# A two-layer graph-attention kernel: x transposed by VectorE flips instead of TensorE, its low part on GpSimd, the adjacency read directly, and new instruction orders

## The reference, cut to what matters

```python
# layer 0: q, k, v = x@Wq.T, x@Wk.T, x@Wv.T + bv
scores = einsum('bqhd,bkhd->bhqk', q, k) * 384**-0.5 + (adj + adj)
p = softmax(where(any(scores != 0, -1), scores, -inf)); p = nan_to_num(p)
x = layernorm(x + (p @ v) @ Wo.T + bo)
# layer 1: q, k, v = x@Wq + bq, x@Wk + bk, x@Wv + bv
scores = einsum('bhqd,bhkd->bhqk', q, k) / sqrt(32) + beta * adj
p = softmax(where(adj > 0, scores, -9e15))
out = layernorm(x + p @ v)
```

## Time and profile before

| what | value |
|---|---|
| median of 3 runs | 2175.8 us (2172.58 to 2176.5) |
| the profiled execution, its own time | 2174.43 us |
| its span, first to last instruction | 2172.6 us |
| PE busy | 2073.7 us, 95% |
| DVE busy | 1859.6 us, 86% |
| ACT busy | 1838.6 us, 85% |
| POOL busy | 1564.2 us, 72% |
| mean share of the DMA engines | 54.8% |

### The profile page before, as it was taken

How to read it: one execution, slowest core, us unless ns; L and a number is a source line. 1 busy time by engine, 2 the same in 40 slices (tenths; PEclk the granted TensorE clock), 3 DMA queues, 4 the chain that set the end, 5 groups by cost and what they waited for, 6 DMA issues and landing times.

```text
span 2172.6 us, 86873 instructions
## 1 busy us (share of the span) xinstructions
PE 2073.7 (95%) x23808; PEld 1911.8 (88%) x23808; DVE 1859.6 (86%) x8451; ACT 1838.6 (85%) x7688; POOL 1564.2 (72%) x2188
## 2 busy tenths in 40 slices
PE   5899999999999999999999999999999999999974
PEld 4799989999999999999999999999998999999963
DVE  2588888998898998898898888898889899889874
ACT  4489888888888888888988888988888988888874
POOL 3667777777777777777777777777777777777752
PEclk8899999999999999999999999999999999999986
DMA  4255565565565565555556556556555556556544
GB/s 124 64 133 143 137 152 144 137 153 135 137 153 135 137 152 140 135 149 144 136 144 153 130 142 154 139 137 153 136 138 153 144 135 152 137 137 153 128 120 105
DMA packets 234778, 300.33 MB, mean 138 GB/s; under 512 B 26704, under 2 KB 226384, under 8 KB 234576
## 3 DMA queue, kind: packets, MB, share of 16 engines
q1 hardware_dynamic: 234576, 298.43, 54.8%
HBM read 46.67 MB, written 25.17 MB: 33 GB/s over the span
## 4 chain that ended last, share of the span: by engine, by line
PE 74%; DVE 11%; issue 8%; POOL 3%; DMA 1%; DVEq 1%; ACT 1%; SPq 0%; POOLq 0%; ACTq 0%
PE r_bank L371 18%; PE r_bank L373 17%; PE r_bank L372 17%; PE s_bank L421 9%; PE r_bank L437 7%; DVE neg_s L699 4%; PE r_bank L354 2%; PE r_bank L449 2%; DVE neg_max L699 1%; DVE x1T_lo L721 1%; PE r_bank L364 1%; DVE flip L715 1%; DMA prob0T<-flip 1%; DVE v L776 1%; DVE sum_neg L748 1%
## 5 line engine op out<-in xcount | busy, mean ns | idle before, releaser
L594 ACT ACTIVATE prob<-neg_s,neg_max 128x128 f32<-128x128 f32 x3072 | 1190.7, 393 | 98.6 <-DVE flip L715 82.0
L699 DVE CUSTOM_DVE_ANT_0 neg_s<-s_bank,bias 128x128 f32<-128x128 f32 x3072 | 668.3, 285 | 67.4 <-PE s_bank L421 64.4
L594 ACT ACTIVATION_READ_ACCUMULATOR prob<-neg_s,neg_max 128x1 f32 x3072 | 592.5, 193 | 0.0
L928 POOL TENSOR_TENSOR prob<-prob,inv_sum 128x512 f32<-128x512 f32 x384 | 389.4, 1042 | 223.6 <-DVE inv_sum L787 223.6
L371 PE MATMUL r_bank<-xT_hi,w_hi 128*128 128x256 f32 x1152 | 328.7, 285 | 20.9 <-DVE xT_lo L721 19.4
L371 PE MATMUL r_bank<-x1T_hi,w_hi 128*128 128x256 f32 x1152 | 337.2, 293 | 10.5 <-DVE x1T_lo L721 8.3
L373 PE MATMUL r_bank<-xT_hi,w_lo 128*128 128x256 f32 x1152 | 327.6, 284 | 0.0
L372 PE MATMUL r_bank<-xT_lo,w_hi 128*128 128x256 f32 x1152 | 327.4, 284 | 0.0
L373 PE MATMUL r_bank<-x1T_hi,w_lo 128*128 128x256 f32 x1152 | 325.5, 283 | 0.0
L372 PE MATMUL r_bank<-x1T_lo,w_hi 128*128 128x256 f32 x1152 | 324.9, 282 | 0.0
L910 POOL TENSOR_TENSOR flip<-neg_s 128x768 f32<-128x768 f32 x128 | 234.9, 1835 | 95.0 <-DMA prob0T<-flip 94.9
(11 more groups left out here) (82 smaller groups left out, 5242.2 us busy)
## 6 DMA issues: line engine op xcount, KB each, us to landing
prob0T<-flip SPq DMA_DIRECT2D x512, 192.0 KB, 3.5
prob1T<-stage SPq DMA_DIRECT2D x512, 192.0 KB, 3.6
x_in<-in_x_dram SPq DMA_DIRECT2D x128, 192.0 KB, 3.6
x_late<-x SPq DMA_DIRECT2D x64, 384.0 KB, 4.2
out_dram<-y SPq DMA_DIRECT2D x128, 192.0 KB, 2.4
adj<-in_adj_dram SPq DMA_DIRECT2D x256, 64.0 KB, 2.4
stage<-in_L_gnn_Wv_dram SPq DMA_DIRECT2D x1, 576.0 KB, 5.7
stage<-in_L_gnn_Wq_dram SPq DMA_DIRECT2D x1, 576.0 KB, 6.6
```

The costliest lines, as they stand in the source:

```text
L594: act.activation(prob[layer][:, h, :], neg_s[layer][:, h, :], ACT.Exp, bias=neg_max[layer][:, h:h + 1], scale=-1.0, accum_out=row_sum[laye ...
L699: dve.tensor_tensor_reduce(neg_s[layer][:, h, :], s_bank[b][:, (h // HC) * N:(h // HC + 1) * N], bias[layer][q.parity][:, g, :], -1.0, BIG ...
L928: pool.tensor_tensor(prob[0][:, hs, :], prob[0][:, hs, :], inv_sum0[:, hs].unsqueeze(2).to_broadcast([P, HC, N]), ALU.mult).then_inc(probn ...
```

## The change

- x is loaded twice. The copy for the residual goes straight into x_bo and bo is added in place. The copy for the transposition goes into x_q: partition block i (32 partitions) holds features 96i to 96i+95 of tokens in blocks of 32, in pieces of 96 floats. DVE transposes its 32x32 blocks into xT, and this is the full transpose. The three weights of layer 0 that multiply x are loaded with their rows in the matching order, two of them from ACT's queue.
- The six transposes of x per body leave PE; two flips of 128x384 join DVE (`flip_x`). ACT's high part reads xT in SBUF with a stride, and the low part (`low_xT`) moves from DVE to POOL, with a strided read too.
- The bias of layer 0 is no longer made: `negate` reads adj with the factor -2, and q is scaled by half.
- RING_USERS loses xt0 and xt1, so it has 26 names, which is no multiple of four, and all orders of work are new. On PE the attention of layer 0's first graph, attend(0, n, 0), moves from the start of the next body to the end of this one. The loop covers bodies 9 to 60.
- Weights are staged in other buffers; POOL splits three of them, at the end of body 0.

```diff
-FIRST, LAST = -1, PAIRS + 3
-LOOP_FROM = 7
-LOOP_N = PAIRS - 1 - LOOP_FROM
+FIRST, LAST = -2, PAIRS + 4
+LOOP_FROM = 9
+LOOP_N = PAIRS - 3 - LOOP_FROM
...
+RING_USERS = ["g1_0", "v0_1", "wo_0", "g1_1", "ot_0", "pv1_1", "v1_0", "g1_2",
+              "g0_0", "g1_3", "g1_4", "pv0_1", "ot_1", "v1_1", "g0_1", "g1_5",
+              "wo_1", "g0_2", "g0_3", "g0_4", "x1t0", "g0_5", "v0_0", "x1t1",
+              "pv0_0", "pv1_0"]
 RING = 4
-assert len(RING_USERS) % RING == 0
...
+            def load_q(q):
+                if q.valid():
+                    sp.wait_ge(xflip_done, q.count(1, 0, 0))
+                    for i in range(NB):
+                        sp.dma_start(x_q[HD * i:HD * (i + 1), :, :],
+                                     x[bass.ds(2 * q.index(), 2)].rearrange("g (j a) d -> a (g j) d", j=NB)[:, :, QD * i:QD * (i + 1)]
+                                     ).then_inc(xq_loaded, 16)
...
+                spread_probs(1, m4, 1)
+                store(m5, 1)
+                load_x(n)
                 spread_probs(0, m1, 1)
+                load_adj1(m1)
...
                     load_adj0(p1)
+                keep_x1(m3)
                 spread_probs(1, m3, 0)
+                store(m4, 0)
+                load_q(p3)
                 spread_probs(0, n, 0)
...
# PE, the whole body as it is now
                 scores(0, n, 0, r)
                 project_qk(1, m2, 0, r)
                 project_v(0, n, 1, r)
                 project_out0(m1, 0, r)
                 project_qk(1, m2, 1, r)
                 transpose_out1(m4, 0, r)
                 scores(1, m3, 1, r)
                 attend(1, m4, 1, r)
                 project_v(1, m2, 0, r)
                 project_qk(1, m2, 2, r)
                 project_qk(0, p1, 0, r)
                 project_qk(1, m2, 3, r)
                 project_qk(1, m2, 4, r)
                 attend(0, m1, 1, r)
                 transpose_out1(m4, 1, r)
                 scores(0, n, 1, r)
                 project_v(1, m2, 1, r)
                 project_qk(0, p1, 1, r)
                 project_qk(1, m2, 5, r)
                 project_out0(m1, 1, r)
                 project_qk(0, p1, 2, r)
                 project_qk(0, p1, 3, r)
                 project_qk(0, p1, 4, r)
                 transpose_x1(m1, 0, r)
                 scores(1, m2, 0, r)
                 project_qk(0, p1, 5, r)
                 project_v(0, p1, 0, r)
                 transpose_x1(m1, 1, r)
                 attend(0, n, 0, r)
                 attend(1, m3, 0, r)
...
# ACT, the end of the body
+                exps(0, n, 1, 8, 10)
                 qk_out(0, p1, 4, r)
+                norm_apply0(m1, 1)
+                exps(1, m2, 0, 0, 2)
                 qk_out(0, p1, 5, r)
                 high_x1T(m1, 1)
+                exps(0, n, 1, 10, 12)
+                high_o0T(n, 0)
...
# DVE, the start and the end of the body
                 inverse_sums0(m1, 1)
                 low_o0T(m1, 0)
                 negate(0, n, 0, (0, 1, 2, 3))
                 flip_probs(0, m1, 1)
...
                 negate(1, m2, 0, (0, 1, 2, 3))
+                values_out(0, p1, 0)
+                low_x1T(m1, 1)
+                abs_max(n, 1)
...
+            def flip_x(q, g):
+                if q.valid():
+                    dve.wait_ge(xq_loaded, q.count(8 * NB, 1, 8 * NB))
+                    dve.wait_ge(xt_lo_done, q.plus(-1).count(1, g, 1))
+                    dve.transpose(xT[:, :, g * N:(g + 1) * N].rearrange("p c (j a) -> p c j a", j=NB),
+                                  x_q[:, g * NB:(g + 1) * NB, :].rearrange("p j (c b) -> p c j b", c=C)
+                                  ).then_inc(xflip_done, 1)
...
# POOL, the body as it is now
                 normalise0(m1, 1)
+                residual0(m1, r)
+                low_xT(p1, 0)
+                low_xT(p1, 1)
                 residual1(m4, 0)
+                inverse_std(0, m1, 0)
+                fold_scores0(n, 0)
                 inverse_std(1, m4, 0)
                 normalise0(n, 0)
+                make_bias1(m1, 0)
                 residual1(m4, 1)
                 inverse_std(0, m1, 1)
+                make_bias1(m1, 1)
+                fold_scores0(n, 1)
                 inverse_std(1, m4, 1)
+                if is_peeled(r, off, 0):
+                    low_weights(WQ1, WK1, WV1)
```

More of the change, by code:

```diff
@@ L32 @@
 NB = N // HD
+QD = D // NB
 PAIRS = NG // 2
@@ L139, in build @@
         neg_half = sb("neg_half", [P, 1])
-        x_in = [sb(f"x_in{b}", [P, 2, D]) for b in range(2)]
+        x_q = sb("x_q", [P, 2 * NB, QD])
         x_bo = [sb(f"x_bo{b}", [P, 2, D]) for b in range(2)]
@@ L144, in build @@
         adj1 = sb("adj1", [P, 2, N])
-        bias = [[sb(f"bias{l}_{b}", [P, 2, N]) for b in range(2)] for l in range(2)]
+        bias1 = [sb(f"bias1_{b}", [P, 2, N]) for b in range(2)]
         qT = [[sb(f"q{l}T_{b}", [P, C, G2]) for b in range(2)] for l in range(2)]
@@ L279, in load_weights, with load_rows @@
                              ).then_inc(w_loaded[i], 16)
-            load_x(Pair(0, 0))
-            load_weights(WV0)
-            load_weights(WQ0)
+            def load_rows(i):
+                for k in range(NB):
+                    sp.dma_start(w_stage[i][HD * k:HD * (k + 1), :, :],
+                                 wts[i][QD * k:QD * (k + 1), :].rearrange("(c b) o -> b c o", c=C)).then_inc(w_loaded[i], 16)
+            load_q(Pair(0, 0))
+            load_rows(WV0)
             for layer, b_ in enumerate((bv0, bv1)):
                 sp.dma_start(bv_row[layer][:], b_.partition_broadcast(P)).then_inc(bv_loaded, 16)
-            load_weights(WK0)
             load_adj0(Pair(0, 0))
@@ L332, in _ @@
         def _(pe):
-            read = [(xt_lo_done, 0, 0, 0, 0)] * 4
+            read = [(v_out[0], 0, 0, 0, 0)] * 4
             s_read = [(neg_done[0], 0, 0, 0, 0)] * HC
@@ L346, in after_loop @@
                         table[i] = (sem_, off - 2, per, g, plus)
-            def transpose_x(q, g, r):
-                if q.valid():
-                    pe.wait_ge(*last_read(read, BANK[f"xt{g}"], r))
-                    read[BANK[f"xt{g}"]] = (xt_lo_done, q.off, 1, g, 1)
-                    pe.wait_ge(x_loaded[q.parity], q.loads(2))
-                    for c in range(C):
-                        mm = pe.transpose(ring(f"xt{g}")[:, c * P:(c + 1) * P],
-                                          x_in[q.parity][:, g, c * P:(c + 1) * P], ident[:])
-                    mm.then_inc(xt_done, 1)
             def transpose_x1(q, g, r):
@@ L607, in body @@
+                exps(1, m3, 0, 4, 8)
+                high_xT(p1, 0)
+                exps(1, m3, 0, 8, 10)
+                high_xT(p1, 1)
+                if is_peeled(r, off, -1):
+                    high_weights(WO0)
                 qk_out(1, m2, 0, r)
-                exps(1, m3, 0, 6, 12)
+                exps(1, m3, 0, 10, 12)
+                exps(0, n, 0, 0, 4)
                 qk_out(1, m2, 1, r)
-                exps(0, n, 0, 0, 4)
+                exps(0, n, 0, 4, 6)
+                out1T_out(m4, 1)
@@ L796, in body @@
                 n = Pair(r, off)
-                m4, m3, m2, m1, p1 = (n.plus(-4), n.plus(-3), n.plus(-2), n.plus(-1), n.plus(1))
-                values_out(0, n, 0)
-                low_x1T(m2, 1)
-                abs_max(m1, 1)
+                m4, m3, m2, m1, p1, p2 = (n.plus(-4), n.plus(-3), n.plus(-2), n.plus(-1), n.plus(1), n.plus(2))
                 inverse_sums0(m1, 1)
-                attention_out1(m4, 0)
                 low_o0T(m1, 0)
@@ L902, in make_bias1, with low_xT @@
                     pool.wait_ge(bias1_steps, q.count(3, g, 2))
-                    pool.tensor_tensor(bias[1][b][:, g, :], adj1[:, g, :], mask1[:], ALU.add).then_inc(bias1_steps, 1)
+                    pool.tensor_tensor(bias1[b][:, g, :], adj1[:, g, :], mask1[:], ALU.add).then_inc(bias1_steps, 1)
+            def low_xT(q, g):
+                if q.valid():
+                    pool.wait_ge(xt_hi_done, q.count(1, g, 1))
+                    if g == 0:
+                        pool.wait_ge(v_done[0], q.count(1, 0, 0))
+                        pool.wait_ge(g_done[0], q.count(3, 0, 0))
+                    m = slice(g * N, (g + 1) * N)
+                    pool.tensor_tensor(*(t.rearrange("p c (a j) -> p c a j", j=NB) if i != 1 else t.rearrange("p c (j a) -> p c a j", j=NB)
+                                        for i, t in enumerate((xT_lo[:, :, m], xT[:, :, m], xT_hi[:, :, m].bitcast(F32)))), ALU.subtract
+                                      ).then_inc(xt_lo_done, 1)
             def fold_scores0(q, g):
```

213 lines of the change are left out of this document (88 added, 125 removed).

## The result

The changed kernel takes 2480.0 us (2478.8 to 2480.7), the kernel before 2175.3 us on the same chip: 1.1405 times as long, 95% interval [1.1391, 1.1418]. The forecast was 2193 us.

What follows compares the result with a forecast made beforehand. PE was taken to bound the kernel: 31.77 us a body plus 1.12 us a turn. Bodies +11.4, turns +2.3 and start +4 gave +17.7 us on 2174.4, 2192.1, so forecast 2193 us; range 2148 to 2214.

Steps and rivals of the forecast that it cites:

- A new wait of PE: Over the body's end, project_qk(1, m2, 0) waits for low_o0T to read pv0_0's bank: 0.58 us per body.
- PE's own time: Six transposes per body leave PE, others get dearer: PE gains 0.39 us, not 0.72, body 31.38 us.
- The turn: DVE's standstill where the loop turns back costs 1.3 us instead of 1.12, 25 times instead of 27: +2.3 us.
- What costs nothing: Flips on DVE, strided high part on ACT, low parts on POOL, bias change: covered by idle time, bodies unchanged.
- pieces of x_q that hold up the spread: Rival: small x_q DMAs delay the spread, layer 0 sets the pace: some +60 us, 2253 us; chance 0.07.
- The adjacency: In layer 0, reading the bias straight from adj and halving q changes factors only; booked at nothing.
- The start: POOL's three weight splits delay the second flip to 66.3 us from 62.08: +4 us (0 to +7).

Runs made afterwards that it cites:

- banks by hand: The changed kernel with one edit: the four shared PSUM banks assigned to the 26 users by a written-out table that avoids the four clashes; 2176.5 us, 1.001.
- the predicted wait alone: Against the kernel with hand-assigned banks (2176.5 us): pv0_0 put back on g1_0's bank, x1t1 on bank 3 in exchange; 2186.8 us, 1.0044.
- the jump moved: The changed kernel with plain bank rotation, its jump by two moved from the body's end to project_out0(m1, 1) (wo_1); 2161.8 us, 0.9935.

## Why the prediction was wrong

Right in sign, far off in size: 18 us forecast, 304 measured. The step that failed is **"A new wait of PE"**. Its mechanism is right, and so is its size (0.63 us against 0.58). In the kernel that has it alone the path through ACT and DVE takes 3.44 us (1255.23 to 1258.67) where 3.46 was forecast, and PE's own steps 2.75 (1.87 us to 1257.10 and 0.88 for the scores) where 2.88 was forecast. The step failed in its reach: it took the rotation to be disturbed over the end of the body alone, where 26 is not a multiple of 4, and laid two paths side by side for that one pair of names. It did not go through the other pairs. But a rotation is only harmless if the orders of the readers fit it everywhere, and the change replaced both: the list of names and the orders of DVE and ACT. In the kernel before wo_1 followed g0_0 on its bank and g0_2 followed g1_3, both read by ACT; now they follow ot_1 and v1_1, which DVE reads late. What the prediction put at nothing by leaving it out, these two hand-overs, measured 1.8 and 1.1 us a body and, each alone, 134 to 163 and 96 us.

The account of the pair of bodies shown above, from the traces. PE's own work is 2 x 31.13 = 62.3 us. The waits are shown as 1.02, 0.43, 1.62 and 1.11 us in the first body and 0.63, 0.40, 1.86 and 1.11 in the second, 8.2 us. But a wait costs more than it shows. For g0_2 in the first body, the last start of PE ahead of the wait and the second start behind it lie 1.68 us apart (1257.15, 1258.83), where neighbouring rows have 0.29: 1.39 us for a wait shown as 1.11. Measured like this, from start to start, the eight waits cost 10.2 us (for the last the 1.39 of the first body is taken, since the clock was low). With 2.5 us for the clock the sum is 75.0 us, and 75.0 were measured.

Against the 64.4 us of the kernel with banks by hand the pair loses 10.6 us, and 30 pairs would make 318 us; measured were 304. Not every pair loses as much: the one from 336.59 to 408.61 takes 72.0 us, the clock is at 0.99 to 1.00 until 400 us, and later too a body now and then takes 36.00 us instead of 38.5 (895.19 to 931.19).

Step by step:

- **PE's own time**: forecast 31.38 us a body, measured 31.13 (above, at the predicted wait alone). The body of 31.44 us with banks by hand comes near the forecast by chance, because it holds 0.3 us of a hand-over. The transposes ahead of scores cost 0.42 and 0.48 us as taken from the earlier trace rows, but PE gains 0.64 us instead of 0.39; where the other 0.25 us come from is not traced.
- **The wait over the body's end**: 0.58 forecast, 0.63 measured, but it lengthens the body by only 0.38 us, and in a body with the turn it replaces a wait that would come later. The kernel that has this one of the four waits takes 2186.8 us. It is the kernel that the sum of the prediction describes (2193 us), and that the two are so near is in part luck: its plain body is 31.82 us instead of 31.96 and its turn 1.0 us instead of 1.3, while the start costs more than forecast.
- **The turn**: 1.3 us forecast. With banks by hand 1.52, with the jump moved 0.3: the standstill of DVE has no price of its own; it costs what PE waits for at the first thing that DVE owes. DVE's standstill lay where forecast, before the reciprocal, but came in two parts (timeline of DVE, banks):

```profile
1214.62 0.23 DVE L794 RECIPROCAL inv_raw<-row_sum 128x12 f32<-128x12 f32 x1 [0.64 <-issue]
...
1218.28 0.08 DVE L709 DVE_READ_ACCUMULATOR2_ANT neg_max<- 128x1 f32 x1 [0.63 <-issue]
```

- **What costs nothing**: the groups of the changed kernel, with the DMAs, next to the earlier trace rows:

```profile
L527 ACT ACTIVATE xT_hi<-xT 128x384 fp32r<-128x384 f32 x128 | 118.8, 931 | 87.5 <-PE r_bank L372 45.8 <-issue 39.5 <-DVE xT L737 2.1
L737 DVE STREAM_TRANSPOSE xT<-x_q 128x384 f32<-128x384 f32 x128 | 66.3, 555 | 6.4 <-DMA x_q<-in_x_dram 4.9 <-POOL xT_lo L914 1.4
L914 POOL TENSOR_TENSOR xT_lo<-xT,xT_hi 128x384 fp32r<-128x384 f32 x128 | 153.6, 1213 | 19.6 <-ACT xT_hi L527 17.4
```
```profile
x_q<-in_x_dram SPq DMA_DIRECT2D x256, 96.0 KB, 2.2
```

  The flip takes 0.555 us (0.44 to 0.55 forecast), the high part 0.93 (0.48 to 0.96), the low part 1.21 (1.0 to 2.0), the pieces of x_q land after 2.2 us (2.4 to 7.2). The kernels with good banks show that the bodies stay as they are. The Trainium skill's 50% for a read with a step ("GPSIMD Engine Reference", "Performance pitfalls for Q7 kernels") is 19% here, 1213 against 1017 ns; but of the two inputs of the low part only xT is read with a step (of 128 bytes), so this does not test the rule on a single read. The Trainium skill's remark on transfers below 512 bytes ("DMA: Bandwidth & Descriptors", "Specifications") does not show in the landing time of 384-byte pieces. The rival built on it, pieces of x_q that hold up the spread, falls.
- **The adjacency**: booked at nothing, brought 6 us, at the turn.
- **The start**: +4 us forecast. With banks by hand the second flip starts at 65.84 us (66.3 forecast, 62.08 before), and PE's waits up to 500 us sum to 47 us against 39: +8 us. Of the 47 us, 4.7 are waits at ot_0 that belong to the turn, so +8 is an upper end.
- With banks by hand the sum is then 60 x (31.44 - 31.77) = -20, turns 25 x 1.52 - 27 x 1.12 = +8, start +8: -4 us. Measured +1.3; the 5 us between are not traced. So the design without its clashes stands about where the kernel before stands, and this holds with DVE's turn moved as well, 2142.2 us against 2139.5.

The sign for which the text argued, a hand-over of a bank that comes late, was the right kind of cause. None of the rivals had more than one such pair.

What stays open: what it takes for the clock to fall in one of two bodies with nearly equal waits; and why the standstill of DVE at the turn vanishes when the turn lies ahead of a negate and behind short statistics steps, while it is whole when a negate, 24 short instructions, runs a few steps ahead of it. The runs show that it does, in both designs, not why.

## What to carry to other kernels

A rotating buffer is a set of dependencies that no line of the code spells out. Whenever its length, its list or the order of its readers changes, write down for each user the previous user of its slot, the engine that reads that one, and what stands ahead of the read on this engine; one pair out of 26 cost 134 us. Go through all pairs, not only those at a jump: the two dearest here were ordinary ones. Give such a ring an explicit table, or place the jump so that it parts the pairs that clash. And the point where a loop turns back is a choice on each engine: rotating DVE's body by two or four steps, with the sequence of work unchanged, brought 29 and 34 us, and 3 us where PE hardly felt the turn. The kernel before with the adjacency read directly and DVE's turn moved is the fastest of this study, 2139.5 us.

## What the runs showed of the hardware

- The standstill of DVE at a loop's turn depends on which instructions stand around the turn: 1.06 us in one piece before, 0.64 + 0.63 us in two, or next to nothing, for the same loop and the same work.
- A wait of PE costs more than the idle time that the profile shows for it: amid plain products 1.39 us for 1.11 shown, measured from start to start. Of the 0.28 us more, 0.10 lie behind the first matmul (0.22 us to the second instead of 0.12).
- The granted clock fell from 2.4 to 1.2 GHz for about 7 us after PE had been idle 1.86 us, with another 1.11 us of idle time inside, and it cost that body 2.5 us. The body before it, with 1.62 and 1.11 us, kept 2.4 GHz. Kernels with one of these two waits kept a mean of 0.974 to 0.981; the one with a wait of 3.3 us a body had 0.932.
- ACT's copy of a 128x384 tile took 931 ns when it read SBUF with a step of 32 elements, against 476 ns from PSUM without one in the kernel before (first row). A copy of 128x1152 from SBUF without a step took 1157 ns in the changed kernel (second row). That is 2.4 ns an element of a row with the step and 1.0 without, so the step costs, and not SBUF:

```profile
L519 ACT ACTIVATE xT_hi<-r_bank 128x384 fp32r<-128x384 f32 x128 | 60.8, 476 | 1.5 <-PE r_bank L354 1.3
L516 ACT ACTIVATE w_hi<-prob 128x1152 fp32r<-128x1152 f32 x2 | 2.3, 1157 | 1.2 <-DMA prob<-in_L_gnn_Wq_dram 1.2
```
